# Feature-major tail of a conv, linear-attention and mixture-of-experts kernel: gates broadcast by DMA, inputs gated on GpSimd, experts summed on TensorE

## The chip, the cores and the metric

The kernel runs on 1 core of a Trainium2 chip. Its time is the device time in microseconds (us) from start to end of the one execution. TensorE is called PE below, VectorE DVE, ScalarE ACT, GpSimd POOL, and SyncE SP; PEld is TensorE loading weights.

## What is computed

For 32 images of 56 x 56 tokens with 32 channels each:

```python
x = x + conv3x3(sign(batchnorm(groupnorm(x))), sign(W) * mean|W|)
t = x.reshape(32, 3136, 32)
# linear attention, 16 heads of 32, on t' = layernorm(t)
q, k = elu(t' @ wq.T + bq) + 1, elu(t' @ wk.T + bk) + 1
v = t' @ wv.T + bv
# k and q each once times cos(pos), once times sin(pos)
kv = einsum('bshx,bshz->bhxz', k_cs, v)
o = einsum('bshx,bhxz->bshz', q_cs, kv) / (q_cs . sum(k_cs) + 1e-5)
t = t + o @ dense_w.T + dense_b
# top-2 of 8 experts, on u = layernorm(t)
p = softmax(u @ router_w + router_b); gates = top-2 of p, scaled to sum 1
t = t + sum over the two experts of gate * (u @ expert_w[e] + expert_b[e])
```

## The kernel before

The program is written by hand for five engines, with semaphores. An image is cut into 28 slots of 112 tokens (`SLOTS`, `PT`): 7 tiles of four groups. Feature-major, a tile is 128 partitions (4 groups x 32 channels) by 112 columns, an image 128 x 784 (`PATCHES`). Token-major it is 112 partitions by 28 x 32.

A start-up part loads the inputs' statistics and the weights. Then each image goes through steps, each with a kind and a number. `schedule()` gives every step a time, in units of which 14 (`PERIOD`) make one period; a period is one image. `SHIFTS` moves a kind on one engine. From both, `iteration(engine, i)` makes the list of one iteration: steps of up to six images stand in one list, since an image lives for about five periods. Each engine walks its list in order (`walk`) and waits in front of a step for the semaphores that it needs. Nothing is reordered at run time, so a step that waits holds everything that is behind it on its engine. Iterations 3 to 28 run in a loop of two at a time.

The steps in the order of one image (lines of the profile):

- XT (L538, L958, L685): SP loads xt in four transfers of 28 rows (L469), PE transposes, DVE binarizes into `nat`, ACT keeps the residual. SP copies `nat` into `shifted` (L483); CV (L547, L968) is the convolution.
- XC, SM1, PN1, XH1, PL1, ZT: the first layer norm. PE centers and turns the image token-major, ACT squares, DVE sums, POOL takes the power -0.5 and scales (L788, L792), ACT and POOL split it into two half-precision parts, PE transposes them back (L563), ACT copies (L706).
- K (14 of them; L571, L711, L989), KX (L580), KT, G (L589): keys and the sums over tokens. Q (14; L596, L716, L995): queries. DN, SU, RC, RL (L605, L613, L1007, L1012): denominators. R and RP (7 each; L622): the reciprocals spread over features, multiplied by DVE (L1017) and by POOL (L810). NM (7; L631, L1023): numerators.
- T2 (4; L642, L644): PE adds the residual `t1b` and the two halves of `pbuf`, and turns the result token-major together with its channel means; ACT copies to `t2` and `mean2` (L756, L758), POOL subtracts the mean (L815). S2, SM2, PN2, XH2, PL2, ZU are the second layer norm, by the same means as the first.
- LG (L650, L1027): router logits. RT (7 steps, DVE): top-2; GT (POOL): gates, 112 x 224.
- F (7; L656): PE computes all eight experts for four slots, tokens on the partitions, into 112 x 1024 of PSUM. DVE multiplies by the gates while it evicts (L1079), POOL sums the eight in three halving additions (L839, L842, L845). OUT: POOL adds `t2` (L833), SP stores (L488).

PSUM is used as a ring of three pairs of banks for the kinds in `RING`, and one bank for those in `MISC`: PE waits in front of a step until the step that had the slot before has been read (`READ`).

## Time and profile before

| | us |
|---|---|
| median of 3 runs | 2708.9 (2705.72 to 2708.95) |
| profiled execution | 2711.49 |
| its span, first to last instruction | 2709.7 |
| PE busy | 2368.0 (87%) |
| DVE busy | 2308.7 (85%) |
| POOL busy | 1864.9 (69%) |
| ACT busy | 1743.9 (64%) |
| DMA queue of SP, share of 16 engines | 9.6% |

The profile is of one execution. Busy times are sums of instructions; waits in front of an instruction aren't counted in. The share of the whole span mixes the start, in which DMA loads and statistics run, with the long middle in which one image follows the other, and with the end. Divided by 32, a busy time is the work for one image. A group of instructions is named by its line, its engine and its operation, with the tile written, the tiles read and their shapes. A float32 matmul counts as two instructions on PE (line 580 has 1792 for 448 steps of two).

### The profile page before, as it was taken

The numbers are of one execution on the slowest core, as the hardware profiler recorded it, in microseconds if no ns is written. First come the engines' busy times: TensorE is split into PE (matmuls) and PEld (weight loads), VectorE is DVE, ScalarE is ACT, GpSimd is POOL, SyncE is SP. The second block draws the span as 40 slices with busy tenths as digits, with TensorE's granted clock in tenths as the row PEclk, the third lists the DMA queues.
The fourth block names the chain that finished last, engine by engine and source line by source line (L and its number), as shares of the span: only waits on it lengthen the run. The fifth ranks groups of instructions, "written<-read, shape, count | busy, mean of one in ns | idle before, by whom it ended". The sixth has DMA issues, their size and how long they took to land.

```text
span 2709.7 us, 57010 instructions
## 1 busy us (share of the span) xinstructions
PE 2368.0 (87%) x19300; PEld 1162.5 (43%) x19300; DVE 2308.7 (85%) x3041; ACT 1743.9 (64%) x2821; POOL 1864.9 (69%) x1479
## 2 busy tenths in 40 slices
PE   3479999899999989998999999899898989999973
PEld 3324444444444444444443444444444444444442
DVE  4458999898998989899898989899898989999973
ACT  0067767676676767666676666677676767777630
POOL 0124777777777777777777777677777867777677
PEclk7589999999999999999999999999999999999995
DMA  8210000000000000000000000000000000000000
GB/s 257 34 15 10 11 16 17 7 12 17 17 17 17 17 17 3 16 17 17 16 16 17 4 14 17 17 16 16 17 14 4 17 17 16 16 11 7 7 7 12
DMA packets 232232, 55.14 MB, mean 20 GB/s; under 512 B 226064, under 2 KB 226944, under 8 KB 231776
## 3 DMA queue, kind: packets, MB, share of 16 engines
q1 hardware_dynamic: 231904, 50.95, 9.6%
q8 instruction: 184, 3.01, 0.5%
q14 instruction: 144, 1.18, 0.2%
HBM read 31.19 MB, written 12.85 MB: 16 GB/s over the span
## 4 chain that ended last, share of the span: by engine, by line
PE 39%; DVE 35%; issue 17%; ACT 4%; POOL 2%; DMA 1%; DVEq 1%; SPq 1%; ACTq 0%; POOLq 0%
DVE kbuf L989 8%; PE ps L605 7%; DVE qbuf L995 6%; PE ps L580 6%; PE ps L571 4%; PE ps L622 4%; PE ps L656 3%; PE ps L596 3%; PE ps L631 3%; DVE prod L1079 2%; DVE route L1054 2%; PE ps L563 2%; DVE rs L1012 2%; DVE nat L958 2%; ACT ebuf L716 2%
## 5 line engine op out<-in xcount | busy, mean ns | idle before, releaser
L711 ACT ACTIVATE ebuf<-ps,small 112x1024 f32<-112x1024 f32 x448 | 498.5, 1113 | 291.9 <-PE ps L571 241.4
L989 DVE SCALAR_TENSOR_TENSOR kbuf<-ps,ebuf 112x1024 f32<-112x1024 f32 x448 | 542.1, 1210 | 109.5 <-ACT ebuf L711 106.4
L810 POOL TENSOR_TENSOR qbuf<-spread_r,qbuf 128x896 f32<-128x896 f32 x224 | 472.2, 2108 | 176.2 <-ACT spread_r L746 176.0
L995 DVE SCALAR_TENSOR_TENSOR qbuf<-ps,ebuf 128x896 f32<-128x896 f32 x448 | 485.2, 1083 | 71.7 <-ACT ebuf L716 50.9
L716 ACT ACTIVATE ebuf<-ps,small 128x896 f32<-128x896 f32 x448 | 451.4, 1008 | 122.9 <-PE ps L596 70.9
L580 PE MATMUL ps<-kbuf,xcs 112*64 112x512 f32 x1792 | 491.0, 627 | 40.5 <-issue 35.3
L788 POOL TENSOR_TENSOR rstd<-varr,power 112x28 f32<-112x28 f32 x64 | 307.3, 4802 | 200.2 <-DVE varr L979 196.7
L631 PE MATMUL ps<-qbuf,gmat 128*64 128x224 f32 x3584 | 388.1, 359 | 37.4 <-DVE pbuf L1023 33.7
L839 POOL TENSOR_TENSOR prod<-prod 112x512 f32<-112x512 f32 x224 | 285.8, 1276 | 103.0 <-DVE prod L1079 103.0
L746 ACT ACTIVATE spread_r<-ps 128x896 f32<-128x896 f32 x224 | 205.5, 917 | 173.4 <-PE ps L622 166.5
L631 PEld LDWEIGHTS ps<-qbuf,gmat 128*64 128x64 f32 x3584 | 237.2, 137 | 155.1 <-DVE pbuf L1023 41.8
L1079 DVE TENSOR_TENSOR prod<-ps,gate 112x1024 f32<-112x1024 f32 x224 | 269.4, 1214 | 32.9 <-POOL gate L829 17.4
L571 PE MATMUL ps<-wk,z 128*112 128x512 f16 x896 | 280.3, 395 | 10.3 <-DVE qbuf L995 3.6
L622 PE MATMUL ps<-rs,sel 128*128 128x448 f16 x896 | 250.2, 368 | 44.6 <-issue 36.6
L1017 DVE TENSOR_TENSOR qbuf<-ps,qbuf 128x896 f32<-128x896 f32 x224 | 241.9, 1080 | 28.8 <-PE ps L622 28.7
L596 PE MATMUL ps<-z,wq 128*128 128x448 f16 x896 | 247.2, 358 | 12.8 <-DVE kbuf L989 7.4
L605 PE MATMUL ps<-qbuf,dmat 128*32 128x448 f32 x1792 | 225.7, 548 | 2.3 <-DVE pbuf L1023 2.2
L798 POOL TENSOR_TENSOR parts<-xn,parts 112x896 f16<-112x896 f32 x64 | 121.2, 1893 | 121.4 <-ACT parts L699 121.4
L706 ACT ACTIVATE z<-ps 128x1568 f16<-128x1568 f16 x128 | 188.9, 1476 | 9.3 <-PE ps L563 9.2
L842 POOL TENSOR_TENSOR prod<-prod 112x256 f32<-112x256 f32 x224 | 164.8, 736 | 17.6
L580 PEld LDWEIGHTS ps<-kbuf,xcs 112*64 112x64 f32 x1792 | 89.4, 136 | 201.9 <-issue 190.5
L563 PE MATMUL ps<-eye,parts 112*64 112x112 f16 (+1 forms) x3840 | 130.3, 219 | 44.8 <-DVE kbuf L989 22.3
(133 smaller groups left out, 3493.8 us busy)
## 6 DMA issues: line engine op xcount, KB each, us to landing
qbuf<-in_x SPq DMA_DIRECT2D x8, 1568.0 KB, 12.4
xt<-in_x SPq DMA_DIRECT2D x128, 98.0 KB
out<-ffn SPq DMA_DIRECT2D x128, 98.0 KB
shifted<-nat SPq DMA_DIRECT2D x128, 52.6 KB, 5.0
qbuf<-in_sel SPq DMA_DIRECT2D x1, 1024.0 KB, 11.7
tabn<-in_tabnc SPq DMA_DIRECT2D x1, 784.0 KB, 13.4
p<-in_p2c SPq DMA_DIRECT2D x1, 528.0 KB, 10.0
tabd<-in_tabdc SPq DMA_DIRECT2D x1, 448.0 KB, 10.7
```

The source lines that it names most:

```text
L571: mm = pe.matmul(o[0:PT, k, :], z1[:, m.par, PT * s:PT * s + PT], wk16[:, :], start=True, stop=True)
L580: mm = pe.matmul(kt_bank[64 * k:64 * k + 64, :], xcs[:, 2 * n + k, :, :].rearrange("p a c -> p (a c)"), kbuf[:, n % 2, DH * k:DH * k + DH] ...
L596: mm = pe.matmul(o[:, k, 0:G * PT], wq16[:, 128 * (k0 + k):128 * (k0 + k) + 128], z1[:, m.par, G * PT * j:G * PT * (j + 1)], start=True, s ...
L605: mm = pe.matmul(o[32 * j:32 * j + 32, 0:HW4], dmat[:, m.par, c, :, :].rearrange("p a h -> p (a h)"), qbuf[:, c, 4 * h + j, :], start=(c = ...
L622: mm = pe.matmul(o[:, k, 0:HW4], sel16[:, 128 * a:128 * a + 128], rs[:, j // 4, :], start=True, stop=True)
L631: mm = pe.matmul(o[64 * v:64 * v + 64, 0:2 * PT].rearrange("p (a t) -> p a t", a=2), gmat[:, m.par, c, :, :].rearrange("p a o -> p (a o)") ...
L711: act.activation(ebuf[0:PT, 0, :].rearrange("p (a b) -> p a b", a=2), o[0:PT, :, :], ACT.Exp, bias=minus_one[0:PT, :]).then_inc(kexp_made, 1)
L716: act.activation(ebuf[:, 1, 0:2 * G * PT].rearrange("p (a b) -> p a b", a=2), o[:, :, 0:G * PT], ACT.Exp, bias=minus_one).then_inc(qexp_ma ...
L810: nc.gpsimd.tensor_tensor(qbuf[:, 2:4, n, :], spread_r[:, :, :], qbuf[:, 2:4, n, :], ALU.mult)\
L989: v.scalar_tensor_tensor(kbuf[:, n % 2, :].rearrange("p (a b) -> p a b", a=2), o[0:PT, :, :], 1.0, ebuf[0:PT, 0, :].rearrange("p (a b) -> ...
L995: v.scalar_tensor_tensor(qbuf[:, k0:k0 + 2, j, :], o[:, :, 0:G * PT], 1.0, ebuf[:, 1, 0:2 * G * PT].rearrange("p (a b) -> p a b", a=2), AL ...
L1079: v.tensor_tensor(prod[:, n % 2, :, :].rearrange("p s (e c) -> p (s e) c", c=C), o[0:PT, :, :].rearrange("p k (s c) -> p (k s) c", c=C), g ...
```

## The change

Behind the numerators everything stays feature-major.

- T2: PE only adds the halves of `pbuf` (a 128 x 64 matrix of ones and zeros, two matmuls for a block of up to 224 columns); DVE adds the residual while it evicts, into `t2f`. Blocks are of two tiles, the fourth of one (`BLOCKS`).
- XD: seven matmuls give the centered image token-major, and beside it the raw router products (160 columns). ACT copies both and squares. S2, POOL's centering, XH2, PL2 and ZU go; SM2 sums all squares at once. POOL's LG scales the raw products by the reciprocal deviation and adds a bias.
- ZF: PE transposes the normed image in float32, ACT copies it to `z2`, SP stores it to DRAM (`z_rows`, 4 transfers of 32 rows). GX: PE transposes the gates, ACT copies them, SP stores them (`g_rows`).
- FF (4 blocks): SP loads z back, four copies for the four groups of partitions (`zrep`), and the gates of two sets of four experts, each expert's row on 32 partitions (`zg`). These are three transfers of 128 partitions x 896 columns (448 KB), for the fourth block half of that. There are two buffers: a block waits until the block two before it was added (`ff_made`). POOL multiplies `zg` by `zrep` in place (128 x 1792), PE multiplies by the expert weights with 32 channels of four experts on the rows, which sums the experts (32 matmuls in an image), DVE adds the result to `t2f`.
- YT: PE transposes `t2f`, ACT copies, SP stores. OUT's addition and all of F go.
- G: `dmat` is now made by one DVE multiply in place of eight small ACT copies.
- The schedule's times and shifts are all new; the SP list has the new steps ZF, GX and FF.

```diff
+    add("ZF", [25.99])
+    add("GX", [31.05])
+    add("FF", [35.56, 37.34, 38.05, 40.07])
+    add("GT", [37.41])
+    add("YT", [40.95])
+    add("OUT", [59.64])
     return sorted(s)
 
...
+                if kind == "ZF":
+                    sp.wait_ge(z_made[1], m.at(1, 1))
+                    rows = z_rows[m.par].rearrange("c (j g t) -> g c j t", g=G, t=PT)
+                    for g in range(G):
+                        src = z2[32 * g:32 * g + 32, :].rearrange("p (j t) -> p j t", t=PT)
+                        sp.dma_start(rows[g], src).then_inc(z_stored, 16)
+                if kind == "GX":
+                    sp.wait_ge(gates_turned, m.at(1, 1))
+                    rows = g_rows[m.par].rearrange("e (s t) -> s e t", t=PT)
+                    for h in range(2):
+                        w = G * HALF[h]
+                        sp.dma_start(rows[16 * h:16 * h + w], gsb[0:EXPERTS * w, h, :]).then_inc(gates_stored, 16)
+                if kind == "FF":
+                    w = BLOCKS[n] * HW4
+                    a = 2 * HW4 * n
+                    sp.wait_ge(z_stored, m.at(64, 64))
+                    wait(sp, ff_made, m.at_from(4, n - 1, 4 * m.par + n + 1))
+                    src = z_rows[m.par, :, a:a + w].unsqueeze(0).to_broadcast([4, C, w])
+                    sp.dma_start(zrep[:, n % 2, 0:w], src).then_inc(zg_in[n % 2], 16)
+                    sp.wait_ge(gates_stored, m.at(32, 32))
+                    for k in range(2):
+                        src = g_rows[m.par, 4 * k:4 * k + 4, a:a + w].unsqueeze(1).to_broadcast([4, 32, w])
+                        sp.dma_start(zg[:, n % 2, k, 0:w], src).then_inc(zg_in[n % 2], 16)
...
-                    tiles = range(2 * n, min(2 * n + 2, TILES))
-                    pe.wait_ge(numer_made, m.at(7, tiles[-1] + 1))
-                    if n == 0:
-                        pe.wait_ge(t1b_made, m.at(1, 1))
-                    for jj, j in enumerate(tiles):
-                        dst = o[0:PT, 256 * jj:256 * jj + 132]
-                        pe.matmul(dst, t1b[:, PT * j:PT * j + PT], eye_mean[:, :], start=True, stop=False)
-                        for a in range(2):
-                            mm = pe.matmul(dst[:, 66 * a:66 * a + 66], pbuf[:, j % 4, a, :], pair_sb[:, :],
-                                           start=False, stop=(a == 1))
+                    w = BLOCKS[n]
+                    k0 = 2 * n % 4
+                    pe.wait_ge(numer_made, m.at(7, 2 * n + w))
+                    for a in range(2):
+                        mm = pe.matmul(o[64 * a:64 * a + 64, 0:w * PT].rearrange("p (j t) -> p j t", t=PT), both_sb[:, :],
+                                       pbuf[:, k0:k0 + w, a, :], start=True, stop=True)
                     mm.then_inc(misc_full, 1)
-                elif kind == "LG":
-                    pe.wait_ge(z_made[1], m.at(2, 2))
-                    for s in range(SLOTS):
-                        mm = pe.matmul(o[0:PT, 0, EXPERTS * s:EXPERTS * s + EXPERTS], z2[:, PT * s:PT * s + PT],
-                                       we16[:, EXPERTS * C:], start=True, stop=True)
+                elif kind == "XD":
+                    pe.wait_ge(t2_made, m.at(4, 2 * n + 2))
+                    for j in range(4 * n, 4 * n + HALF[n]):
+                        k, jj = ((j // 2, j % 2), (0, j - 4))[n]
+                        mm = pe.matmul(o[0:PT, k, 160 * jj:160 * jj + 160], t2f[:, m.par, PT * j:PT * j + PT],
+                                       eye_center[:, 128:288], start=True, stop=True)
                     mm.then_inc(ring_full, 1)
-                elif kind == "F":
-                    for k in range(4):
-                        s = 4 * n + k
-                        mm = pe.matmul(o[0:PT, k // 2, 256 * (k % 2):256 * (k % 2) + 256], z2[:, PT * s:PT * s + PT],
-                                       we16[:, 0:EXPERTS * C], start=True, stop=True)
+                elif kind == "ZF":
+                    pe.wait_ge(ones_made, m.at(1, 1))
+                    for j in range(TILES):
+                        mm = pe.transpose(o[:, j // 4, PT * (j % 4):PT * (j % 4) + PT],
+                                          xn[1][:, G * j:G * j + G, :].rearrange("p s c -> p (s c)"), eye[0:PT, 0:PT])
+                    mm.then_inc(ring_full, 1)
+                elif kind == "GX":
+                    pe.wait_ge(gate_made, m.at(1, 1))
+                    for h in range(2):
+                        w = 32 * HALF[h]
+                        mm = pe.transpose(o[0:w, PT * h:PT * h + PT], gate[:, 128 * h:128 * h + w], eye[0:PT, 0:PT])
+                    mm.then_inc(misc_full, 1)
+                elif kind == "FF":
+                    w = BLOCKS[n]
+                    pe.wait_ge(zg_made, m.at(4, n + 1))
+                    for c in range(2):
+                        rhs = zg[:, n % 2, c, 0:w * HW4].rearrange("p (j g t) -> p g j t", g=G, t=PT)
+                        for g in range(G):
+                            mm = pe.matmul(o[32 * g:32 * g + 32, 0:w * PT].rearrange("p (j t) -> p j t", t=PT), wff[:, c, :],
+                                           rhs[:, g], start=(c == 0), stop=(c == 1))
+                    mm.then_inc(misc_full, 1)
+                elif kind == "YT":
+                    pe.wait_ge(ff_made, m.at(4, 4))
+                    for j in range(TILES):
+                        mm = pe.transpose(o[0:PT, j // 4, 128 * (j % 4):128 * (j % 4) + 128],
+                                          t2f[:, m.par, PT * j:PT * j + PT], eye)
...
+                elif kind == "GX":
                     act.wait_ge(misc_full, no + 1)
...
+                    wait(act, gates_stored, m.at(32))
+                    for h in range(2):
+                        w = 32 * HALF[h]
+                        last = act.activation(gsb[0:w, h, :], o[0:w, PT * h:PT * h + PT], ACT.Copy)
+                    last.then_inc(gates_turned, 1)
...
+                elif kind == "YT":
+                    act.wait_ge(ring_full, no + 1)
+                    wait(act, out_stored, m.at(64))
+                    for h in range(2):
+                        a, w = 16 * h, 4 * HALF[h]
+                        last = act.activation(ffn[:, a:a + w, :], o[0:PT, h, 0:w * C].rearrange("p (s c) -> p s c", c=C),
+                                              ACT.Copy)
+                    last.then_inc(out_made, 1)
...
+                    if ln:
+                        nc.gpsimd.memset(xn[1][:, :, C - 1:C], 1.0).then_inc(ones_made, 1)
+                elif kind == "LG":
+                    slots = [PT, SLOTS, EXPERTS]
+                    logits = route[:, 0, :].rearrange("p (s e) -> p s e", e=EXPERTS)
+                    pool.wait_ge(rstd_made[1], m.at(1, 1))
+                    nc.gpsimd.tensor_tensor(logits, raw[:, :].rearrange("p (s e) -> p s e", e=EXPERTS),
+                                            rstd[1][:, :].unsqueeze(2).to_broadcast(slots), ALU.mult).then_inc(logits_scaled, 1)
+                    pool.wait_ge(logits_scaled, m.at(1, 1))
+                    nc.gpsimd.tensor_tensor(logits, logits, router_b[:, :].unsqueeze(1).to_broadcast(slots), ALU.add)\
+                        .then_inc(logits_made, 1)
...
+                elif kind == "FF":
+                    w = BLOCKS[n] * HW4
+                    pool.wait_ge(zg_in[n % 2], m.at(96, 48 * (n // 2) + 48))
+                    nc.gpsimd.tensor_tensor(zg[:, n % 2, :, 0:w], zg[:, n % 2, :, 0:w],
+                                            zrep[:, n % 2, 0:w].unsqueeze(1).to_broadcast([128, 2, w]), ALU.mult)\
+                        .then_inc(zg_made, 1)
...
+                elif kind == "T2":
+                    dve.wait_ge(misc_full, no + 1)
+                    if n == 0:
+                        dve.wait_ge(t1b_made, m.at(1, 1))
+                    a, w = 2 * PT * n, BLOCKS[n] * PT
+                    v.tensor_tensor(t2f[:, m.par, a:a + w], o[:, 0:w], t2f[:, m.par, a:a + w], ALU.add).then_inc(t2_made, 1)
...
+                elif kind == "FF":
+                    dve.wait_ge(misc_full, no + 1)
+                    a, w = 2 * PT * n, BLOCKS[n] * PT
+                    v.tensor_tensor(t2f[:, m.par, a:a + w], o[:, 0:w], t2f[:, m.par, a:a + w], ALU.add).then_inc(ff_made, 1)
```

How the steps stand on the engines. On SP, in the middle of the loop, before (L469 loads xt, L483 makes shifted, L488 stores the output):

```order
L469 DMA xt<-in_x 28x14x64
L469 ISA
L469 DMA xt<-in_x 28x14x64
L469 ISA
L469 DMA xt<-in_x 28x14x64
L478 REGISTER_ALU
L483 DMA shifted<-nat 32x29x29 x4
L485 REGISTER_ALU
L488 ISA
L488 DMA out<-ffn 28x14x64
L488 ISA
```

and now, from the store of an image's gates (L518) on; L525 loads z, L529 the gates for the same block:

```order
L518 DMA g_rows<-gsb 16x8x112
L518 DMA g_rows<-gsb 12x8x112
L522 REGISTER_ALU
L444 ISA
L525 DMA zrep<-z_rows 128x1x896
L526 REGISTER_ALU
L529 DMA zg<-g_rows 128x1x896 x2
L444 ISA
L525 DMA zrep<-z_rows 128x1x896
L529 DMA zg<-g_rows 128x1x896 x2
L444 ISA
L525 DMA zrep<-z_rows 128x1x896
```

followed by the shifted copies of a later image between the third block's loads and the fourth's:

```order
L501 REGISTER_ALU
L506 DMA shifted<-nat 32x29x29 x4
L444 ISA
L525 DMA zrep<-z_rows 128x1x448
L529 DMA zg<-g_rows 128x1x448 x2
```

So the loads of an image stand behind the store of its gates, and one block behind the other.

On POOL, before, around the second layer norm's power (L788; L839, L842 and L845 are the product sums, L810 is an RP step, L815 the centering):

```order
L835 REGISTER_ALU
L839 TENSOR_TENSOR prod<-prod 112x4x128
L841 REGISTER_ALU
L842 TENSOR_TENSOR prod<-prod 112x4x64
L844 REGISTER_ALU
L845 TENSOR_TENSOR ffn<-prod 112x128
L809 REGISTER_ALU
L810 TENSOR_TENSOR qbuf<-spread_r,qbuf 128x2x448
L787 REGISTER_ALU
L788 TENSOR_TENSOR rstd<-varr,power 112x28
L422 REGISTER_ALU
L792 TENSOR_TENSOR xn<-xc,rstd 112x28x31
```

and now (L919 is a block's gating, L870 the power, L884 and L887 the logits, L903 an RP step):

```order
L918 REGISTER_ALU
L919 TENSOR_TENSOR zg<-zg,zrep 128x1792
L869 REGISTER_ALU
L870 TENSOR_TENSOR rstd<-varr,power 112x28
L875 TENSOR_TENSOR xn<-xn,rstd 112x28x31
L879 MEMSET xn 112x28
L884 TENSOR_TENSOR route<-raw,rstd 112x224
L887 TENSOR_TENSOR route<-route,router_b 112x224
L919 TENSOR_TENSOR zg<-zg,zrep 128x2x448
L902 REGISTER_ALU
L903 TENSOR_TENSOR qbuf<-spread_r,qbuf 128x2x448
```

The second layer norm of the next image now stands between the gatings of blocks 2 and 3.

On PE, now, the fourth block (L720, 32x112) in the list of its iteration, behind the transposes of ZF (L705); L672 is RP, L630 KX, L621 K, L726 YT, L646 Q, L683 NM:

```order
L703 REGISTER_ALU
L705 MATMUL ps<-eye_center,xn 128x112 x7
L716 REGISTER_ALU
L720 MATMUL ps<-zg,wff 32x112 x8
L672 MATMUL ps<-rs,sel 128x448 x2
L630 MATMUL ps<-kbuf,xcs 64x512 x2
L584 REGISTER_ALU
L621 MATMUL ps<-wk,z 112x512 x2
L726 MATMUL ps<-eye_center,t2f 112x128 x7
L646 MATMUL ps<-z,wq 128x448 x2
L683 MATMUL ps<-qbuf,gmat 64x224 x8
```

and, further on, the gates of the next image (L712) in the next iteration, behind an R and a T2 step (L692):

```order
L692 MATMUL ps<-pbuf,both_sb 64x224 x2
L646 MATMUL ps<-z,wq 128x448 x2
L584 REGISTER_ALU
L672 MATMUL ps<-rs,sel 128x448 x2
L584 REGISTER_ALU
L709 REGISTER_ALU
L712 MATMUL ps<-eye_center,gate 128x112
L712 MATMUL ps<-eye_center,gate 96x112
L584 REGISTER_ALU
```

Between the two stand the steps K8 to K13, KX6 to KX12, Q0 to Q5, R4, R5, RP3, RP4, CV, NM1 to NM3, XC, XT, YT and two T2; before, the expert matmuls (L656) stood one by one among such steps.

## Rows read from the trace of the kernel before

**Rows 1.** The page, part 1: busy us (share of the span) xinstructions.

```profile
PE 2368.0 (87%) x19300; PEld 1162.5 (43%) x19300; DVE 2308.7 (85%) x3041; ACT 1743.9 (64%) x2821; POOL 1864.9 (69%) x1479
```

**Rows 2.** Stretches: length, busy of PE, PEld, DVE, ACT, POOL, PEclk, DMA, GB/s.

```profile
100.00:200.00 100.00, 59.06 (x353) 22.67 (x355) 45.23 (x70) 44.32 (x67) 26.27 (x16) 0.72 0.17 19
...
1000.00:1200.00 200.00, 185.03 (x1613) 91.28 (x1615) 180.89 (x234) 140.54 (x234) 148.92 (x121) 0.99 0.09 17
```

**Rows 3.** Line 1027 (once per image): ns min/median/max, first and last start in us.

```profile
L1027 DVE COPY route<-ps x32: 378/380/393, 306.7 to 2675.8; 112x224 f32<-112x224 f32 x32
```

**Rows 4.** Groups by line, PE, what goes: shapes xcount | busy us, mean ns | idle before.

```profile
L656 PE MATMUL ps<-we,z 128*112 128x256 f16 x896 | 145.4, 288 | 10.2 <-DVE prod L1079 10.2
...
L563 PE MATMUL ps<-eye,parts 112*64 112x112 f16 (+1 forms) x3840 | 130.3, 219 | 44.8 <-DVE kbuf L989 22.3 <-issue 12.7 <-POOL parts L798 9.8
...
L644 PE MATMUL ps<-pair_sb,pbuf 128*112 128x66 f32 x896 | 116.0, 252 | 0.0
...
L642 PE MATMUL ps<-eye_mean,t1b 128*112 128x132 f32 x448 | 91.9, 287 | 7.5 <-DVE pbuf L1023 7.1 <-ACT mean L758 0.3
...
L650 PE MATMUL ps<-we,z 128*112 128x8 f16 x896 | 51.2, 193 | 1.7 <-ACT z L706 1.7
```

**Rows 5.** Groups by line, PE, next to what comes.

```profile
L631 PE MATMUL ps<-qbuf,gmat 128*64 128x224 f32 x3584 | 388.1, 359 | 37.4 <-DVE pbuf L1023 33.7 <-ACT den L734 0.9 <-ACT xres L685 0.5
...
L605 PE MATMUL ps<-qbuf,dmat 128*32 128x448 f32 x1792 | 225.7, 548 | 2.3 <-DVE pbuf L1023 2.2 <-ACT mean L758 0.2
...
L552 PE MATMUL ps<-eye_center,t 128*112 128x128 f32 x448 | 55.8, 278 | 1.3 <-DVE t L968 0.7 <-DVE kbuf L989 0.7
...
L538 PE MATMUL ps<-eye_center,xt 112*128 112x112 f32 x224 | 34.4, 271 | 37.9 <-DVE pbuf L1023 24.5 <-DVE small L944 9.0 <-ACT xres L685 4.4
```

**Rows 6.** Groups by line, DVE: the products that go, an eviction of 224 columns.

```profile
L1079 DVE TENSOR_TENSOR prod<-ps,gate 112x1024 f32<-112x1024 f32 x224 | 269.4, 1214 | 32.9 <-POOL gate L829 17.4 <-POOL ffn L845 10.5 <-PE ps L656 3.5
...
L1023 DVE TENSOR_TENSOR pbuf<-ps,tabn 128x224 f32<-128x224 f32 x224 | 85.1, 380 | 5.6 <-PE ps L631 5.5
```

**Rows 7.** Groups by line, POOL.

```profile
L810 POOL TENSOR_TENSOR qbuf<-spread_r,qbuf 128x896 f32<-128x896 f32 x224 | 472.2, 2108 | 176.2 <-ACT spread_r L746 176.0
...
L788 POOL TENSOR_TENSOR rstd<-varr,power 112x28 f32<-112x28 f32 x64 | 307.3, 4802 | 200.2 <-DVE varr L979 196.7
...
L792 POOL TENSOR_TENSOR xn<-xc,rstd 112x868 f32<-112x868 f32 x64 | 105.8, 1653 | 7.1 <-POOL rstd L788 4.1
```

**Rows 8.** Stretches, columns as in rows 2: start-up loads twice, then xt alone.

```profile
20.00:30.00 10.00, 0.58 (x7) 0.37 (x4) 2.59 (x6) 0.00 (x0) 0.00 (x0) 0.65 1.05 376
...
60.00:70.00 10.00, 4.58 (x34) 4.37 (x33) 9.48 (x24) 0.00 (x0) 0.00 (x0) 0.70 1.02 290
...
1248.50:1249.50 1.00, 1.00 (x8) 0.51 (x5) 1.00 (x2) 0.49 (x1) 1.00 (x3) 1.00 0.86 194
```

**Rows 9.** DMA issues: out<-in, engine, op xcount, KB each, median us to landing.

```profile
shifted<-nat SPq DMA_DIRECT2D x128, 52.6 KB, 5.0
...
small<-in_gamma SPq DMA_DIRECT2D x1, 0.5 KB, 2.1
```

**Rows 10.** Groups by line, PE: K, KX, Q, R with RP, CV steps.

```profile
L580 PE MATMUL ps<-kbuf,xcs 112*64 112x512 f32 x1792 | 491.0, 627 | 40.5 <-issue 35.3 <-DVE kbuf L989 5.2
...
L571 PE MATMUL ps<-wk,z 128*112 128x512 f16 x896 | 280.3, 395 | 10.3 <-DVE qbuf L995 3.6 <-DVE kbuf L989 3.2 <-ACT z L706 1.6
...
L622 PE MATMUL ps<-rs,sel 128*128 128x448 f16 x896 | 250.2, 368 | 44.6 <-issue 36.6 <-DVE rs L1012 6.6 <-DVE kbuf L989 0.8
...
L596 PE MATMUL ps<-z,wq 128*128 128x448 f16 x896 | 247.2, 358 | 12.8 <-DVE kbuf L989 7.4 <-DVE qbuf L1017 2.1 <-DVE qbuf L995 0.6
...
L547 PE MATMUL ps<-shifted,conv_w 128*128 128x448 bf16 (+1 forms) x256 | 60.4, 361 | 10.2 <-DMA shifted<-nat 9.4 <-DVE t L968 0.8
```

345 lines of the change are left out of this document (167 added, 178 removed), and 16 rows, old and new, of the table SHIFTS.

## The prediction

> **What bounds the kernel now.** I read the busy times first. PE is busy 2368.0 us and DVE 2308.7 us of 2709.7 [rows 1], so 74.0 and 72.1 us for each of the 32 images; POOL has 58.3. Then the stretches: in the middle of the run PE is busy 92.5% and DVE 90% at a granted clock of 0.99, while between 100 and 200 us, where PE works only 59% of the time, the clock is 0.72 [rows 2]. The copy of the router's logits runs once per image, first at 306.7 us, last at 2675.8 us [rows 3]: a period of 2369.1 / 31 = 76.4 us, 306.7 us before it and 33.9 after. So two engines of nearly equal load set a period close to their own work, and no DMA matters: the sum has to be made for the period, with the two ends apart. The profiled execution took 2711.49 us for a span of 2709.7; the median of the runs is 2708.9, so a span becomes a median by taking off 0.8.
>
> **What the engines save.** PE loses, per image, the expert matmuls (145.4 / 32 = 4.5 us), the logit matmuls (1.6), the token-major output of the attention (2.9 + 3.6) and half of the half-precision transposes (130.3 / 64 = 2.0) [rows 4]: 14.7 us. It gains seven centering matmuls of 160 columns (the 128-column kind costs 55.8 / 224 = 0.25 us, so 7 x 0.31 = 2.2), 16 transposes at 34.4 / 224 = 0.15 us (2.5), eight T2 matmuls at 388.1 / 1792 = 0.22 (1.7), and 28 full-size expert matmuls in groups of 32 columns, bounded by half and by all of the 0.25 us of the denominator's matmuls with twice the columns; I take 4.5 us, near the lower end because the moving columns are half [rows 5]. Together 10.9: PE goes from 74.0 to 70.2 us. DVE loses its products (269.4 / 32 = 8.4 us) and gains eight additions at 0.38 us (3.0) [rows 6]; the rest of its edits about cancel: 72.1 to 66.7. ACT loses more copies than it gains and was not near the bound. POOL loses the product sums, the centering and PL2, and gains 3.5 block multiplies of 1792 elements, at twice the 2.11 us of 896 elements 4.2 us each, 14.8 us [rows 7]; it ends below where it was. On these sums alone the period would be 76.4 x 70.2 / 74.0 = 72.5 us.
>
> **What the change adds on a path.** The gates of an image now go PE (GX), ACT, a store to DRAM, a load copied over 128 partitions, POOL, and PE again (FF). The loads of a block are three of 448 KB; a block is 1.376 MB, an image has 3.5 of them, 4.82 MB. There are two buffers. Block 2 is issued when block 0 has been added, block 3 when block 1 has. Until the previous image's gates have been used and this image's GX has run on PE, none can start: SP waits for the gates' store ahead of block 0's gate loads. And PE takes its steps in a written order: GX stands before FF of the same image, and the next GX behind it. So GX, loads, POOL, last FF, the PE work up to the next GX is a loop, once per image, however idle the engines are.
>
> How fast do the loads run? In the start, loads with 112 outermost rows keep 16 engines busy (share 1.02) and move 290 GB/s in pieces of 3584 bytes, 18.1 GB/s for each engine; the best stretch has 376 GB/s, 23.5 each. A transfer of xt, with 28 outermost rows, keeps 0.86 of the 16 busy, which is 14 of them, and moves 194 GB/s, 13.9 each [rows 8]. 14 is the largest number up to 16 that divides 28, and 16 divides 112. The new loads have 4 outermost copies (of z) or 4 outermost rows (of the gates) on the DRAM side. By that reading each runs on four engines, the same four every time. I take this as the case, because the one row whose count isn't a multiple of 16 shows it. The Trainium skill, page "DMA: Bandwidth & Descriptors", section "Why a DMA increments its semaphore by 16 and not by 1", says the same: the engine count is the largest up to 16 that divides the outermost sizes of both sides, and a leading broadcast of c copies confines the transfer to c engines. The trace agrees with it in the 14 of 28.
>
> The rate of one engine I take from the row with the same piece size, 18.1 GB/s; the ends are 23.5 and 13.9. Then a block takes 1.376 / 0.0725 = 19.0 us and an image 66.4 us of loading, one block behind the other. The Trainium skill gives about 27 GiB/s (29 GB/s) for an engine (same page, "Specifications"); by it an image would load in 41.5 us and the end would be an estimated 2980 us. The rows stay below that figure.
>
> The loop, per image: 2 us for GX, its copies and the issues (an estimate between 1 and 5: two transposes are 0.3, and a store like that of the small inputs lands in 2.1 us, beside which z's load already runs); 66.4 us of loads; 2 us for the shifted copies, which SP issues between blocks 2 and 3 (they land in 5.0 us alone) and 2.1 us for the last landing [rows 9]: 72.5. POOL has a second path: blocks 0 to 2 landed at 2 + 57.0 + 2.1, block 2's multiply 4.2, then PN2, which stands between blocks 2 and 3 on POOL (4.8 + 1.65), and two logit passes (0.6 each, between the 0.43 that 1.65 for 868 elements gives for 224 and twice that): 73.0 [rows 7]. The later counts. Then block 3's multiply 2.1, its matmuls and DVE's addition 0.9: 76.0. Behind it PE has, up to the next GX: 6 K steps (280.3 / 448 = 0.63 each, 3.8), 7 KX (1.10, 7.7), 6 Q (0.55, 3.3), 4 R or RP (0.56, 2.2), two convolution halves (60.4 / 32 = 1.9), 3 NM (388.1 / 224 = 1.73, 5.2), XC 1.7, 13 transposes 2.0, two T2 0.9 [rows 10, 5]: 28.7 us. DVE's work there is less. At the 92.5% of the middle of the run that is 31.0. Period: 107.0 us.
>
> Sum: 306.7 to the first gates, 31 x 107.0 = 3317, less 40 since the stretch from FF to GX empties in the last two periods (by about 15 and 25), plus 80 behind the last GX (73.0 of loads less PN2's 7.7, block 3, transposes, copies, and a store of 4 us, together 76 to 84): 3664. As a median: **3660 us**.
>
> What hides nothing: z's store and the xt loads run in the 31 us in which the four engines are free. If they were slower they would cost at once only beyond that. If the loads were fast, PE would be late next, at 72.5 us.
>
> **Rivals.**
> *Four engines, at the best rate.* At 23.5 GB/s each a block takes 14.6 us and an image 51.2. POOL's path is the later: 2 + 43.9 + 2.1 + 4.2 + 6.5 + 1.2 = 59.9, period 93.9, end 306.7 + 2911 - 40 + 65 = 3240. For it: only four engines pull, and the first stage loads shared DRAM with others. Against it: the long stage loads, in the same pieces, never held it.
> *Four engines that hinder each other.* At 13.9 GB/s the image takes 86.9 us, period 127.0, end 306.7 + 3937 - 40 + 101 = 4300. For it: all four write at the same place of their own quarter of the partitions, in step, and xt's 28 partitions get only 13.9 each. Against it: xt's pieces are of 256 bytes, which costs by itself. The Trainium skill has a rule for this ("SBUF — State Buffer", section "Door 1: The DMA port swizzle"): partitions 32 apart share one port of 27.2 GB/s. No run here separates that from the piece size.
> *All sixteen engines.* If 128 destination rows decide, the loads move 290 GB/s: a block takes 4.7 us, the loop closes in well under 70 us, and PE's sum is the bound: 72.5 us instead of 76.4. Then 2709.7 - 31 x 3.9 = 2589, plus 20 for the longer way of the last image: 2610, faster than before. It decides from the point at which an image's loads take less than about 30 us. For it: nothing in the trace has an outermost count of 4. Against it: the 0.86.
> *The clock.* PE now waits about 30 us in an image and is 66% busy, between the 59% that had a clock of 0.72 and the 92.5% at 0.99 [rows 2]. At 0.72 the 28.7 us become 40, and 31 x 9 = 280 us come on top of any case with four engines. I count it to the ranges, as PE is dense in that stretch itself.
>
> **How the numbers follow.** Forecast 0.42, best rate 0.30, hindered 0.18, sixteen engines 0.08, something between 0.02. The likeliest is 3660 with a range of its own of 3450 to 3950 (the start of the loop, the clock). For 8 in 10 the range must reach over both rate cases: 3000 lies below the best rate with a stretch from FF to GX that is shorter than I sum, 4300 takes half of the hindered case; outside are the sixteen engines and the other half. Faster by over 0.2% (about what a measurement of this kernel can tell from no change) needs the sixteen engines or a loop under 76: 0.09. Within 0.2%: 0.01. Slower: 0.90.
>
> **What would show it.** Right: the DMA row shows a share near 0.25 for some two thirds of each period; the copy from issue to landing of zrep and zg takes 15 us and more; POOL's multiply waits for the DMA of zg, longest of all waits; PE and DVE fall to about 65% busy; the period is 107 us by the once-per-image instructions; POOL's multiply takes 4.2 us. Wrong in the mechanism: a share near 1 in short bursts and waits of POOL for the loads of a few us. Wrong in size only: the same picture with GB/s other than 72 while the loads run.

## The result and the profile after

| | before | after |
|---|---|---|
| median, us | 2708.93 (4 runs) | 3334.28 (3330.94 to 3338.82, 4 runs) |
| ratio of the times | | 1.231, 95% interval 1.229 to 1.233 |
| period of an image | 76.4 | 95.7 |

The changed kernel is 625 us slower. Its page, part 1, to set against [rows 1], and part 3, the queues (packets, MB, share of 16 engines):

```profile
PE 2496.6 (75%) x17768; PEld 1103.9 (33%) x17768; DVE 2045.6 (61%) x3016; ACT 1614.3 (48%) x2213; POOL 1612.8 (48%) x839
...
q1 hardware_dynamic: 321376, 221.21, 23.4%
```

PE's share fell from 87% to 75% and DVE's from 85% to 61%: no engine bounds the kernel any more. The once-per-image instruction that answers to [rows 3] is now the scaling of the logits on POOL:

```profile
L884 POOL TENSOR_TENSOR route<-raw,rstd x32: 572/573/578, 285.3 to 3252.4; 112x224 f32<-112x224 f32 x32
```

(3252.4 - 285.3) / 31 = 95.7 us, against 76.4 before. 31 x 19.3 = 598 of the 620 us between the two spans (3329.2 and 2709.7) are the period; the rest is a start 21 us shorter and an end 43 us longer. The chain of waits gives the place (us in total, times, longest):

```profile
POOL zg L919 <- DMA zg<-g_rows: 858.4, 101, 20.6
...
DVE t2f L1164 <- PE ps L720: 444.6, 67, 28.4
PE ps L720 <- POOL zg L919: 423.9, 68, 23.9
```

POOL waits 858 us for the gates and features to land, PE waits for POOL, DVE for PE. While the loads run (stretches of 5 us, columns as in rows 2):

```profile
1585.00:1590.00 5.00, 4.54 (x68) 2.76 (x64) 1.91 (x4) 4.39 (x6) 0.34 (x1) 1.00 0.27 102
1590.00:1595.00 5.00, 4.95 (x40) 1.32 (x38) 4.86 (x6) 3.17 (x4) 0.00 (x0) 1.00 0.26 103
1595.00:1600.00 5.00, 1.65 (x9) 0.60 (x8) 2.75 (x3) 4.18 (x7) 2.37 (x1) 0.98 0.26 101
1600.00:1605.00 5.00, 3.35 (x20) 1.01 (x22) 1.53 (x3) 0.08 (x1) 5.00 (x4) 0.50 0.25 100
```

The DMA share stands at a quarter: four engines of sixteen, at 102 / 4 = 25.5 GB/s each. In the last row the granted clock is 0.50 (1.2 of 2.4 GHz), behind a stretch in which PE worked 1.65 of 5 us. One cycle of the loop, by POOL's multiplies in its timeline (start, us, ..., idle before it and its releaser):

```profile
1499.43 3.96 POOL L919 TENSOR_TENSOR zg<-zg,zrep 128x1792 f32<-128x1792 f32 x1 [12.86 <-DMA zg<-g_rows]
1513.04 3.97 POOL L919 TENSOR_TENSOR zg<-zg,zrep 128x1792 f32<-128x1792 f32 x1 [5.81 <-DMA zg<-g_rows]
1529.41 3.96 POOL L919 TENSOR_TENSOR zg<-zg,zrep 128x1792 f32<-128x1792 f32 x1 [7.26 <-DMA zg<-g_rows]
1541.14 2.12 POOL L919 TENSOR_TENSOR zg<-zg,zrep 128x896 f32<-128x896 f32 x1
1597.63 3.97 POOL L919 TENSOR_TENSOR zg<-zg,zrep 128x1792 f32<-128x1792 f32 x1 [12.29 <-DMA zg<-g_rows]
```

and by SP's issues in the same cycle (start, us that the issues took SP; the rows left out load the fourth block and `xt` and store `z_rows` and the output):

```profile
1507.56 21.22 SPq L506 DMA_DIRECT2D shifted<-nat  x4
...
1579.30 1.47 SPq L518 DMA_DIRECT2D g_rows<-gsb  x2
1580.98 0.56 SPq L525 DMA_DIRECT2D zrep<-z_rows  x1
1582.12 1.24 SPq L529 DMA_DIRECT2D zg<-g_rows  x2
```

From the multiply of the fourth block to the store of the next gates pass 1579.30 - 1541.14 = 38.2 us without a load, from the store to the first multiply 18.3 us, then 13.6, 16.4 and 11.7: 98.2 us in this cycle, 95.7 in the mean. The first of SP's rows, the four shifted copies, took SP 21.22 us to issue.

### The profile page after: what moved, and what is told of

Read it like the earlier page. It is cut to its first block, busy times and chain, and to the rows that moved or that the text cites. A ratio compares the mean times of both kernels' runs of the same rounds, so it can differ in the third digit from the quotient of the medians.

```text
span 3329.2 us, 52538 instructions
## 1 busy us (share of the span) xinstructions
PE 2496.6 (75%) x17768; PEld 1103.9 (33%) x17768; DVE 2045.6 (61%) x3016; ACT 1614.3 (48%) x2213; POOL 1612.8 (48%) x839
## 4 chain that ended last, share of the span: by engine, by line
issue 43%; POOL 27%; PE 12%; DVE 8%; DMA 6%; ACT 2%; SPq 1%; POOLq 0%; DVEq 0%; ACTq 0%
POOL qbuf L903 9%; POOL rstd L870 6%; POOL zg L919 5%; DMA zg<-g_rows 5%; DVE kbuf L1065 3%; PE ps L683 2%; POOL xn L875 2%; POOL xcs L898 2%; PE ps L655 2%; PE ps L630 2%; PE ps L621 2%; PE ps L720 1%; ACT ebuf L777 1%; DVE den L1090 1%; POOL parts L891 1%
## 5 line engine op out<-in xcount | busy, mean ns | idle before, releaser
L919 POOL TENSOR_TENSOR zg<-zg,zrep 128x1792 f32<-128x1792 f32 (+1 forms) x128 | 447.5, 3496 | 858.7 <-DMA zg<-g_rows 858.4
L903 POOL TENSOR_TENSOR qbuf<-spread_r,qbuf 128x896 f32<-128x896 f32 x224 | 470.3, 2100 | 201.8 <-ACT spread_r L807 201.7
L630 PE MATMUL ps<-kbuf,xcs 112*64 112x512 f32 x1792 | 530.2, 686 | 6.6 <-DVE kbuf L1065 6.6
L720 PE MATMUL ps<-zg,wff 128*32 128x224 f32 (+1 forms) x2048 | 176.6, 485 | 423.9 <-POOL zg L919 423.9
L621 PE MATMUL ps<-wk,z 128*112 128x512 f16 x896 | 303.5, 424 | 192.0 <-ACT spread_r L807 161.5
L683 PE MATMUL ps<-qbuf,gmat 128*64 128x224 f32 x3584 | 419.1, 380 | 6.5 <-POOL qbuf L903 5.0
L870 POOL TENSOR_TENSOR rstd<-varr,power 112x28 f32<-112x28 f32 x64 | 307.2, 4800 | 129.3 <-DVE varr L1060 129.2
L1164 DVE TENSOR_TENSOR t2f<-ps,t2f 128x224 f32<-128x224 f32 (+1 forms) x128 | 45.7, 357 | 444.6 <-PE ps L720 444.6
L683 PEld LDWEIGHTS ps<-qbuf,gmat 128*64 128x64 f32 x3584 | 257.8, 146 | 175.3 <-issue 78.9
L646 PE MATMUL ps<-z,wq 128*128 128x448 f16 x896 | 280.7, 400 | 9.8 <-ACT spread_r L807 5.9
L720 PEld LDWEIGHTS ps<-zg,wff 128*32 128x32 f32 x2048 | 71.0, 144 | 522.2 <-issue 340.6
L672 PE MATMUL ps<-rs,sel 128*128 128x448 f16 x896 | 230.7, 357 | 4.8 <-DVE kbuf L1065 2.0
L621 PEld LDWEIGHTS ps<-wk,z 128*112 128x112 f16 x896 | 107.2, 140 | 366.4 <-ACT spread_r L807 174.2
L630 PEld LDWEIGHTS ps<-kbuf,xcs 112*64 112x64 f32 x1792 | 108.1, 151 | 214.1 <-issue 183.8
```

The lines of the kernel that those rows point to most:

```text
L621: mm = pe.matmul(o[0:PT, k, :], z1[:, m.par, PT * s:PT * s + PT], wk16[:, :], start=True, stop=True)
L630: mm = pe.matmul(kt_bank[64 * k:64 * k + 64, :], xcs[:, 2 * n + k, :, :].rearrange("p a c -> p (a c)"), kbuf[:, n % 2, DH * k:DH * k + DH] ...
L646: mm = pe.matmul(o[:, k, 0:G * PT], wq16[:, 128 * (k0 + k):128 * (k0 + k) + 128], z1[:, m.par, G * PT * j:G * PT * (j + 1)], start=True, s ...
L683: mm = pe.matmul(o[64 * v:64 * v + 64, 0:2 * PT].rearrange("p (a t) -> p a t", a=2), gmat[:, m.par, c, :, :].rearrange("p a o -> p (a o)") ...
L720: mm = pe.matmul(o[32 * g:32 * g + 32, 0:w * PT].rearrange("p (j t) -> p j t", t=PT), wff[:, c, :], rhs[:, g], start=(c == 0), stop=(c == 1))
L870: nc.gpsimd.tensor_tensor(rstd[ln][:, :], varr[ln][:, :], power[0:PT, 0:SLOTS], ALU.pow)\
```

## The experiments

Twelve kernels ran. Each edit is made in the changed kernel; periods come from the same once-per-image instruction, first to last, over 31. The changed kernel has 3334 us and 95.7, the one before 2709 and 76.4. e3, e11 and e14 leave out part of the work.

| kernel | time, us | runs | period |
|---|---|---|---|
| e2: loads cut by columns, four outermost | 3416 | 1 | 98.4 |
| e4: GX two units earlier | 3100 | 1 | 88.3 |
| e1: loads with 32 rows outermost | 2788 | 2 | 79.1 |
| e3: an eighth of the columns loaded | 2771 | 1 | 78.7 |
| e5: e1, GX two units earlier | 2854 | 2 | 81.1 |
| e6: e1, multiply in two halves | 2806 | 4 | 79.5 |
| e7: e1 with both | 2849 | 4 | 80.8 |
| e8: e1, all top-2 steps later, GX one unit earlier | 2839 | 4 | 80.5 |
| e9: e1, three top-2 steps later | 2810 | 4 | 79.5 |
| e12: e1, multiply on VectorE | 2814 | 4 | 79.8 |
| e14: e1, fourth block's multiply cut to an eighth | 2644 | 2 | 74.4 |
| e11: e1, all multiplies cut to an eighth | 2589 | 1 | 72.7 |

### Is it the four engines? (e1, e2)

e1 splits each load so that 32 rows stand outermost (the count that POOL waits for follows):

```diff
-                    src = z_rows[m.par, :, a:a + w].unsqueeze(0).to_broadcast([4, C, w])
-                    sp.dma_start(zrep[:, n % 2, 0:w], src).then_inc(zg_in[n % 2], 16)
+                    for g in range(4):
+                        sp.dma_start(zrep[32 * g:32 * g + 32, n % 2, 0:w], z_rows[m.par, :, a:a + w])\
+                            .then_inc(zg_in[n % 2], 16)
...
+                    for e in range(EXPERTS):
+                        q = slice(32 * (e % 4), 32 * (e % 4) + 32)
+                        src = g_rows[m.par, e, a:a + w].unsqueeze(0).to_broadcast([32, w])
+                        sp.dma_start(zg[q, n % 2, e // 4, 0:w], src).then_inc(zg_in[n % 2], 16)
```

> The same bytes as in the changed kernel, but each block comes in twelve transfers of 32 partitions (outermost count 32 on both sides) in place of three of 128 partitions with an outermost count of 4. Theory A (the loads run on four engines and their time stands in the loop GX, loads, POOL, FF, next GX): the DMA share rises well over 0.25 while the loads run, to 0.8 or more, a block takes about 7 us instead of 13.5, and the period falls from 95.7 us to 2 + 3 x 7.2 + 2.1 + 4.2 + 6.5 + 1.2 + 2.1 + 0.9 + 36 = 77, PE's own bound being 73 to 78: about 2750 us. Theory B (POOL's 4 us multiplies and the order of POOL's list set the period, the loads are hidden beside them): about 3330 us. Theory C (the rate is that of the bytes from DRAM, whatever the number of engines): 100 GB/s stay, 3330 us or more because SP issues 42 transfers in place of 12.

Measured: 2787.65 us (2786.58 to 2788.72, 2 runs), ratio to before 1.029 (1.026 to 1.032). While the first two blocks load:

```profile
1605.00:1610.00 5.00, 4.34 (x105) 3.15 (x107) 2.86 (x8) 4.43 (x6) 2.10 (x1) 1.00 0.71 198
1610.00:1615.00 5.00, 4.96 (x40) 1.73 (x39) 2.92 (x5) 4.04 (x5) 2.03 (x1) 1.00 0.87 235
```

and POOL's wait for the same bytes:

```profile
POOL zg L921 <- DMA zg<-g_rows: 162.9, 36, 10.9
```

858 us of waiting became 163. The share is 0.71 and 0.87 of sixteen engines where it was a quarter, and the same bytes with the same multiplies take away 547 of the 625 us.

e2 makes twelve transfers too, but cuts columns and leaves four outermost copies or rows (the gates in the same way):

```diff
+                    for c in range(0, w, w // 4):
+                        src = z_rows[m.par, :, a + c:a + c + w // 4].unsqueeze(0).to_broadcast([4, C, w // 4])
+                        sp.dma_start(zrep[:, n % 2, c:c + w // 4], src).then_inc(zg_in[n % 2], 16)
```

> Also twelve transfers for a block, but cut by columns: all 128 partitions, a quarter of the columns each, outermost count 4 as in the changed kernel. The bytes are the same, the pieces are 896 bytes. Theory A: still four engines, share 0.25, the period no shorter than 95.7 us, rather longer since pieces of 896 bytes are slower: 3330 to 3600 us. If more and smaller transfers as such are what helps in the other experiment, it is as fast as that one, about 2750 us.

Measured: 3416.28 us (1 run), POOL's wait for the loads 982.8 us. While the loads run the DMA share is 0.27 at 92 GB/s (1645 to 1655 us); over the middle of the run, pauses included, it is 0.25, against 0.23 in the changed kernel. So it is not the number of transfers: what counts is how many rows stand outermost.

### Is it the loop? (e4)

```diff
-    add("GX", [31.05])
+    add("GX", [28.95])
```

> Only one number of the schedule is changed: GX at 28.95 instead of 31.05, so that PE transposes the gates about 12 us of its work earlier in its list. The gates are ready by then (POOL's last gate pass ends 13 us before GX's store is issued). Theory A: the loop loses these steps, period 95.7 - 12 = 84 us, about 2960 us. Theory B: the loads start earlier but POOL's order is unchanged: within 50 us of 3330 us.

Measured: 3099.64 us (1 run), period 88.3, POOL's wait for the loads 410.8 us. With no byte less to load, 235 us go by moving two matmuls in PE's order. That is the loop: in the changed kernel the gates were ready on POOL at 1566.3, 13 us ahead of their store.

```profile
1565.59 0.69 POOL L915 TENSOR_TENSOR gate<-route 112x224 f32<-112x224 f32 x1
```

The gain is 7.4 us an image, not the 11.7 expected. In a cycle of e4 the stretch from the fourth multiply to the store is 23.9 us (1535.96 to 1559.86) instead of 38.2. But the step from the second multiply to the third is 19.9 us instead of 16.4: the first block is multiplied by 1583.0, PE reaches its matmuls in the written order only at 1589.3, and the third block's loads wait for its buffer until 1591.8, 12.8 us behind the start of the first multiply where it was 6.2. Once the gates come early, another place of the same list holds the loads.

### What is left when the loads are fast? (e3, e5)

e3 loads only the first eighth of the columns of each block.

```diff
-                    sp.dma_start(zrep[:, n % 2, 0:w], src).then_inc(zg_in[n % 2], 16)
+                    sp.dma_start(zrep[:, n % 2, 0:w // 8], src[:, :, 0:w // 8]).then_inc(zg_in[n % 2], 16)
...
```

> Of each block's z and gates only the first eighth of the columns is loaded (the rest of the two buffers is set to zero once), so most of the expert output is left out; POOL, PE and DVE do all their work. Theory A: the loads all but vanish from the loop, 12 us less per block; the period falls to PE's bound of 73 to 78 us: 2650 to 2780 us. Theory B: POOL still multiplies as long as before, 3330 us.

Measured: 2771.38 us (1 run). POOL waits 25 us for the loads in all, and the time is only 17 us below e1: what e1's loads still cost is small. But without them the kernel is still 62 us slower than before, where the prediction had PE's own work as the bound, at 72.5 us an image. A second cause was open.

e5 is e1 with the one-line edit of e4.

> The loads on sixteen engines, and the step that turns and stores the gates moved two units earlier in the written order. Loads theory: what is left of the loop in the run with sixteen engines is the wait of GpSimd's first multiply in each image (4.6 us of the 79 us period); with the gates stored earlier it goes, and the time falls from 2788 to some 2650 to 2700. Floor theory: the run with only an eighth of the loads still had a period of 78.7 us, so that wait is slack that another wait takes over; then the time is 2770 to 2790.

Measured: 2853.76 us (2 runs), 66 us slower than e1. Neither theory held. POOL's wait for the loads fell to 21.8 us, but PE stands still for the gates before GX, and NM behind it for ACT's copy of them (idle is the number behind the bar):

```profile
L685 PE MATMUL ps<-qbuf,gmat 128*64 128x224 f32 x3584 | 429.3, 386 | 26.5 <-ACT gsb L838 20.5 <-POOL qbuf L905 5.8 <-DVE t2f L1115 0.3
...
L714 PE MATMUL ps<-eye_center,gate 112*128 112x112 f32 x32 | 9.5, 297 | 30.3 <-POOL gate L917 30.3
```

These were 6.6 and 12.9 us in e1; the two account for 37 of the 66 us. The earlier place pays only while the loads are the bound.

### GpSimd beside VectorE (e6, e7, e8, e9)

In e1, POOL and DVE around the top-2 steps (two timelines, start and us):

```profile
1564.93 0.66 POOL L889 TENSOR_TENSOR route<-route,router_b 112x224 f32<-112x224 f32 x1
1565.55 2.10 POOL L921 TENSOR_TENSOR zg<-zg,zrep 128x896 f32<-128x896 f32 x1
1567.60 2.10 POOL L905 TENSOR_TENSOR qbuf<-spread_r,qbuf 128x896 f32<-128x896 f32 x1
1569.64 2.15 POOL L900 TENSOR_TENSOR xcs<-xn,tabk 112x448 f32<-112x448 f32 x2
1571.76 2.07 POOL L905 TENSOR_TENSOR qbuf<-spread_r,qbuf 128x896 f32<-128x896 f32 x1
```

```profile
1566.31 3.64 DVE L1140 TENSOR_TENSOR route<-route,rmax 112x224 f32<-112x224 f32 x1
1569.98 1.01 DVE L1144 TENSOR_TENSOR route<-route,first 112x224 f32<-112x224 f32 x1
1571.03 0.39 DVE L1146 TENSOR_REDUCE rmax<-route 112x28 f32<-112x224 f32 x1
1571.33 1.21 DVE L1067 SCALAR_TENSOR_TENSOR kbuf<-ps,ebuf 112x1024 f32<-112x1024 f32 x1
1572.46 1.61 DVE L1149 TENSOR_TENSOR route<-route,rmax 112x224 f32<-112x224 f32 x1
```

The same comparison takes 0.39 us ten microseconds later. Here it starts beside the fourth block's multiply, and ends at 1569.95, 0.3 us behind the end of the instruction after that (1567.60 + 2.10 = 1569.70); L1149 ends 0.2 us behind POOL's (1571.76 + 2.07). L1067, which reads one operand from PSUM, keeps its 1.21 us. PE's timeline has the price, two waits of 3.7 us together (the idle time in brackets):

```profile
1572.60 0.64 PE L623 MATMUL ps<-wk,z 128*112 128x512 f16 x2 [2.15 <-DVE kbuf L1067]
1574.83 1.72 PE L728 MATMUL ps<-eye_center,t2f 128*112 128x128 f32 x7 [1.59 <-DVE t2f L1166]
```

The Trainium skill ("SBUF — State Buffer", section "SBUF: two separate sides") has a rule for that: a VectorE instruction with two SBUF inputs and a GpSimd instruction that reads SBUF hold a shared pair of ports for the whole instruction, and the later one blocks. These rows agree with it, and show one thing more: the instruction that waits did not get in where POOL went from one instruction to the next (1567.6).

e6 is e1 with each multiply written as two instructions:

```diff
-                    nc.gpsimd.tensor_tensor(zg[:, n % 2, :, 0:w], zg[:, n % 2, :, 0:w],
-                                            zrep[:, n % 2, 0:w].unsqueeze(1).to_broadcast([128, 2, w]), ALU.mult)\
+                    for k in range(2):
+                        nc.gpsimd.tensor_tensor(zg[:, n % 2, k, 0:w], zg[:, n % 2, k, 0:w], zrep[:, n % 2, 0:w], ALU.mult)\
...
```

> The loads on sixteen engines, and GpSimd's multiply of two sets of 896 elements written as two instructions of 896. Port theory: a VectorE instruction with both operands in SBUF waits until GpSimd's running instruction ends; with halves that take 2 us the mean of the top-2 comparison (route from route and rmax) falls from 1.88 us to 1.1 or less, the period by 1 to 2 us, the time from 2788 to about 2730 to 2760. Rival, the VectorE instructions are long for another reason, or waiting twice for a half costs as much as once for the whole: the comparison stays above 1.6 us and the time at 2780 to 2795.

Measured: 2805.86 us (4 runs), the comparison 1.96 us in the mean where e1 has 1.88. A miss: I had taken the 4 us multiplies for the partner. The rows above show another, the fourth block's, of 2.1 us, with the next instruction right behind it. In e6 its two halves take 2.24 us together, back to back, and the comparison beside them still 3.64.

e7 is e6 with GX at 28.95.

> Both edits together: sixteen engines, gates stored earlier, multiply split. If both theories hold, the period comes near the sum of TensorE's work, 73 to 76 us, and the time is 2600 to 2700, below the kernel before. If only the split helps, 2730 to 2760; if neither, 2770 to 2790.

Measured: 2848.7 us (4 runs), above all three of the times expected. Neither edit helped by itself, nor together.

e8 shifts the top-2 steps in the lists of DVE and ACT (ACT's from 0.60 to 1.60 in the same way), and GX by one unit:

```diff
-    add("GX", [31.05])
+    add("GX", [30.0])
...
-               "RC": 1.78, "RL": 0.43, "RT": 0.55, "SM1": 1.14, "SM2": 1.56, "T2": 0.23, "XT": 0.33},
+               "RC": 1.78, "RL": 0.43, "RT": 1.55, "SM1": 1.14, "SM2": 1.56, "T2": 0.23, "XT": 0.33},
```

> Sixteen engines, gates stored one unit earlier, and the seven top-2 steps one unit later in VectorE's and ScalarE's order. Order theory: the last block's addition stands on VectorE behind top-2 steps that GpSimd's multiplies stretch, and TensorE waits for it in front of the output transpose; with the top-2 steps later that wait (44 us in sum in the run with an eighth of the loads) falls below 20 us, and the time to 2700 to 2750. Rival, the wait only moves on to the gates, which then come later and hold the loads: 2780 or more.

Measured: 2838.98 us (4 runs). The wait in front of the output transposes fell from 46.6 to 1.0 us, as expected, but the key matmuls' wait for DVE rose from 64 to 107 us, and the gates' transposes wait 26.0 us instead of 12.9.

e9 moves only the first three top-2 steps:

```diff
-    add("RT", [24.95, 24.96, 25.35, 26.72, 26.98, 27.12, 28.08])
+    add("RT", [26.08, 26.10, 26.30, 26.72, 26.98, 27.12, 28.08])
```

> Sixteen engines; of the top-2 steps only the first three stand later on VectorE and ScalarE (one more key eviction and the last block's addition come ahead of them); gates' step and the rest unchanged. Theory of the place: in the run with sixteen engines the comparison stands beside four GpSimd instructions in a row (1565.55 to 1573.8) and takes 3.64 us, and TensorE waits 2.15 us for the key eviction behind it and 1.59 us for the addition behind that, 3.7 us an image. With both ahead of the steps, TensorE's waits for the key eviction fall from 64 us to under 20, those for the addition from 47 to under 15, the comparison stays long or shortens as the train ends, and the time goes from 2788 to 2700 to 2740. Rival, the gates come later by as much and something else takes the wait over: 2770 to 2800.

Measured: 2809.62 us (4 runs). Again the wait in front of the transposes is gone and the key matmuls wait 128 us instead of 64: now eight top-2 instructions stand between two key evictions, where e1 has four, and one of them (L1144) took 3.06 us beside POOL. The stretched instructions are still there, and PE waits for whatever stands behind them.

### Taking the multiply away, and moving it (e11, e14, e12)

e11 multiplies only the first eighth of each block's columns:

```diff
-                    nc.gpsimd.tensor_tensor(zg[:, n % 2, :, 0:w], zg[:, n % 2, :, 0:w],
+                    nc.gpsimd.tensor_tensor(zg[:, n % 2, :, 0:w // 8], zg[:, n % 2, :, 0:w // 8],
...
```

> Sixteen engines, all loads full, but GpSimd multiplies only the first eighth of the columns of each block, so most gate values reach the expert matmuls without the features. Leaves GpSimd's 15 us of multiplies an image out but for some 3. Theory that GpSimd's new multiplies lengthen VectorE's two-operand instructions and so hold TensorE: the comparison falls from 1.88 us to near 1.3 (the other GpSimd instructions of the row stay), and the time to 2720 to 2750. Rival, the multiplies have no part in what is left: 2775 to 2790.

Measured: 2589.35 us (1 run); period (2541.4 - 287.3) / 31 = 72.7 us. Far more than either theory had: the multiplies cost some 200 us, with all loads still running. DVE's groups in e11 (busy, mean ns):

```profile
L1097 DVE TENSOR_TENSOR rs<-den,r_high 64x224 f16<-64x224 f32 x128 | 62.4, 487 | 2.9
L1140 DVE TENSOR_TENSOR route<-route,rmax 112x224 f32<-112x224 f32 x64 | 49.6, 776 | 2.2
```

and in e1:

```profile
L1140 DVE TENSOR_TENSOR route<-route,rmax 112x224 f32<-112x224 f32 x64 | 120.2, 1879 | 2.2
L1097 DVE TENSOR_TENSOR rs<-den,r_high 64x224 f16<-64x224 f32 x128 | 109.5, 855 | 2.9
```

DVE as a whole is busy 2022.0 instead of 2178.4 us with the same instructions.

e14 cuts the multiply of the fourth block alone:

```diff
-                    nc.gpsimd.tensor_tensor(zg[:, n % 2, :, 0:w], zg[:, n % 2, :, 0:w],
+                    q = w if n < 3 else w // 8
+                    nc.gpsimd.tensor_tensor(zg[:, n % 2, :, 0:q], zg[:, n % 2, :, 0:q],
...
```

> Sixteen engines, GpSimd multiplies three blocks whole and of the fourth only the first eighth, so a seventh of the tokens keeps gate values that were not multiplied. With all four blocks so cut the time was 2589 us, with none 2788. Theory of the place: nearly all of the 200 us comes from the fourth block's 2.1 us, which stands in the row of GpSimd instructions beside the top-2 comparison, in front of the key eviction and the addition that TensorE waits for; then this run takes 2590 to 2650, and the comparison 1.0 us or less. Theory of the amount: each of the 14 us of multiplies an image costs its share; the fourth block is 2.1 of 14, so 30 us go, and the time is 2750 to 2770.

Measured: 2643.75 us (2 runs), ratio to before 0.975 (0.973 to 0.978). Of some 198 us, 144 hang on the 2.1 us of the fourth block, a seventh of the multiplied elements: the theory of the place holds. The other 54 us go only when the three larger multiplies are cut too. In e14's timelines POOL has a gap behind the short multiply, and the comparison falls into it (POOL, then DVE):

```profile
1571.08 0.42 POOL L922 TENSOR_TENSOR zg<-zg,zrep 128x112 f32<-128x112 f32 x1
1572.46 2.19 POOL L905 TENSOR_TENSOR qbuf<-spread_r,qbuf 128x896 f32<-128x896 f32 x1 [0.95 <-ACT spread_r L809]
```

```profile
1571.87 0.39 DVE L1141 TENSOR_TENSOR route<-route,rmax 112x224 f32<-112x224 f32 x1
```

0.39 us instead of 3.64; the mean is 748 ns instead of 1879. PE's wait for key evictions falls from 64 to 28 us and the one in front of the transposes from 47 to 6, 77 us together. In the cycle shown for e1 the transposes stood behind two waits and took 1.72 us; here they follow without one:

```profile
1576.42 0.93 PE L728 MATMUL ps<-eye_center,t2f 128*112 128x128 f32 x7
```

PE's 17768 instructions were busy 2284.7 us instead of 2347.3, 63 us less, at a mean granted clock of 0.958 instead of 0.932. So a wait costs twice, in idle time and in the lower clock behind it, and the two sums make 140 of the 144 us. A rival is that POOL simply had less to do and its later steps came sooner: its busy time fell by 48 us, but PE's wait for POOL in front of the expert matmuls only from 41 to 36. The product rs, which stands beside the large multiplies, stays at 845 ns: what its stretching costs is at most part of the other 54 us.

e12 gives the whole multiply to DVE, each block right ahead of where PE needs it:

```diff
+    add("FM", [34.84, 36.95, 37.72, 39.45])
...
+                elif kind == "FM":
+                    dve.wait_ge(zg_in[n % 2], m.at(384, 192 * (n // 2) + 192))
+                    v.tensor_tensor(zg[:, n % 2, :, 0:w], zg[:, n % 2, :, 0:w],
+                                    zrep[:, n % 2, 0:w].unsqueeze(1).to_broadcast([128, 2, w]), ALU.mult)\
+                        .then_inc(zg_made, 1)
```

> Sixteen engines, and the whole multiply of gates by features made by VectorE instead of GpSimd, each block just ahead of where TensorE needs it; the same numbers are computed. The run with an eighth of the multiply had 2589 us, so GpSimd's multiplies cost about 200 us, 6.2 us an image; this run tells whether that is GpSimd's hindering of VectorE or the work itself. Theory of hindering: VectorE's other instructions get short again (the comparison near 0.8 us, the product for rs near 0.5), VectorE pays 3.5 x 1.9 = 6.6 us an image on top of 63.2 and stays under TensorE's 71 to 73, and the time is 2630 to 2690, below the kernel before. Rival, the work itself or its place is the cost: VectorE's 1.9 us blocks hold TensorE's evictions as GpSimd did, time 2720 to 2800.

Measured: 2813.72 us (4 runs), ratio to before 1.040 (1.038 to 1.042). rs is back to 487 ns and a multiply takes 1.81 us in the mean, as expected, but the comparison still takes 1.11 us in the mean, beside POOL's other instructions, and PE waits 111 us for the multiplies themselves, where it waited 41 for POOL's:

```profile
L723 PE MATMUL ps<-zg,wff 128*32 128x224 f32 (+1 forms) x2048 | 116.0, 345 | 110.9 <-DVE zg L1161 110.9
```

The work is a cost on either engine in this order. No kernel that leaves nothing out came below the one before; a POOL order in which the fourth block's multiply stands clear of the top-2 steps was not tried.

## Why the prediction was right in sign and 10% high

**The loop over four engines: right.** A share of 0.25 to 0.27, the longest of all waits at POOL's multiply, PE and DVE idle with it: as forecast. From the issue of the first z load (1580.98) to the multiply that waits for its block pass 16.7 us, for the 15 and more forecast. e1 takes away 87% of the loss, e4 moves it by order alone. DVE fell to 61% busy, but PE stayed at 75 and not 65: its instructions took 2496.6 / 32 = 78.0 us an image for the 70.2 forecast, at the lower clock.

**The rate of an engine: the term that was mis-sized.** The forecast took 18.1 GB/s, from the start-up stage in which all sixteen engines load; it measured 25.5 with four at work, and 13.5 us for a block instead of 19.0. In e1 the same pieces move at 198 GB/s for a share of 0.71, which is 11.4 engines at 17.4 each. So an engine had less in e1, where eleven and more work on these pieces, than where four do, and the rival with the best rate (23.5, time 3240) named that reason: only four pull. The number at work is not all of it, as the start-up stretch of 376 GB/s had all sixteen busy at 23.5 each [rows 8]; what else counts there no run tells. The four engines did not halve each other's rate: the rival of 13.9 GB/s fell. The 27 GiB/s (29 GB/s) that the Trainium skill gives for an engine ("DMA: Bandwidth & Descriptors", "Specifications") is nearer to the measured 25.5 than my 18.1.

**What stands around the loads: 8 us short.** With 25.5 GB/s the prediction's own sum for POOL's path would be 15.6 + 13.5 + 13.5 + 11.9 from the store to the fourth multiply, and 36.0 from there to the next store: 90.5 us. The cycle shown has 18.3, 13.6, 16.4, 11.7 and 38.2, together 98.2. In the first, z's load is issued 1.7 us behind the store and the gates' first load 2.8 us behind it. In the third, the DMA share is 0.32 to 0.41 at 69 to 99 GB/s between 1515 and 1530: the shifted copies run beside the block's loads. In the last, PE idles 2.4 us in front of a T2 step (1561.41) and has a granted clock of 0.72 in the 5 us around it, with 0.93 or 1.00 from there to the store. What each of these costs no run separates. So 107.0 falls by 16.5 to 90.5 through the rate, rises by 7.7 to this cycle's 98.2, and the mean cycle is 2.5 shorter: 95.7. That is 31 x 11.3 = 350 us below the forecast. A start 21 us shorter and an end 37 longer than summed leave the 334 us between the two spans, 3664 and 3329.2. The measured 3334 us lie in the range of 3000 to 4300, but below the 3450 to 3950 that the likeliest case had for itself, and nearer to the rival at 3240. With the right rate alone the same sum would end at some 3135 us (306.7 + 31 x 90.5 - 40 + 63, an estimate), 6% low. That the two errors go opposite ways is luck.

**"If the loads were fast, PE would be late next, at 72.5 us": wrong, by place.** e1 and e3 stand at 79 us. The sum of PE's work was nearly right, as e11's 72.7 shows, with PE busy 2277.3 / 32 = 71.2 us for the 70.2 forecast; DVE has 63.2 for 66.7. What was missed is that a multiply of forecast length (4.0 us, said 4.2) on an engine with room to spare stretches its neighbour's instructions, and does so in front of what PE waits for. The rival of sixteen engines fell with the share of 0.25, and its price with e1: the loads are spread over 11 to 14 engines there, and the time is 2788 us, not 2610.

**The clock.** 0.89 in the middle of the run against 0.99 before, with rows at 0.50 behind waits: a cost of waiting, as the rival had it. PE's instructions were busy 149 us more than the same ones in e1 (2496.6 and 2347.3), part of it in stretches where the loads are the later path. In the stretch behind the last block, where the rival had put 9 us an image and 280 in all, the cycle shown is 2.2 us longer than forecast.

## What to carry to other kernels

Before a broadcast load goes into a loop, count what stands outermost on both sides: four copies or four rows meant four DMA engines here, whatever the bytes, and 32 rows outermost a share of 0.71 to 0.87 of sixteen. A rate for one engine that is read while all of them load (18.1 and 23.5 GB/s here) need not be what it does with few at work (25.5); take it as a lower end only. And an engine that has time left is not free: look at which of its neighbour's instructions its new work stands beside, and who waits behind those.

## What the hardware showed beyond that

- A DVE instruction with both operands in SBUF took 3.64 us instead of 0.39 beside two POOL instructions back to back, and ended 0.3 us behind the second. It did not get in between them.
- SP itself is held: issuing the four shifted copies behind loads on four engines took 21.22 us, against 3.18 in e1 (at 1627.52). The two gates' loads of the second block, behind four loads, took 9.26 us (at 1584.81). It isn't only few engines that do it: in the start of the kernel before, six loads of 1568 KB took SP 43.3 us to issue (from 18.89). What is full there no run tells.
- Twelve transfers in pieces of 896 bytes, in place of three in pieces of 3584, cost e2 82 us (3416 for 3334), with 92 GB/s for 102 while they run; which of the two counts it doesn't separate. e1 has as many transfers and isn't bound by them.
